# A larger memset behind each scattered DMA until the last rows are placed, and a waited small one per tile after that, in a mixture-of-experts kernel

## The chip, the cores and the metric

The kernel runs on one core of one Trainium2 chip. The metric is the device time of one execution in microseconds (us). Engines are named as the profile names them: PE is TensorE (PEld its weight loads), DVE VectorE, ACT ScalarE, POOL GpSimd, SP SyncE.

## What is computed

x is (16, 512, 512): 8192 tokens of 512 numbers. Cut to what matters, the reference is

```
z1 = einsum('bfi,bir->bfr', x, v) / 512          # low rank 16, per batch
z  = einsum('bfr,bor->bfo', z1, u) / 16
g  = gelu(einsum('bfi,oi->bfo', x, W) + fc_bias + z + b)
prob = softmax(g @ w_router + b_router)          # 16 experts
mask = the 4 largest of prob
h  = relu(einsum('nd,ebd->neb', g, w1b) + b1b)   # 16 blocks of 128
y  = einsum('neb,ebd,ne->nd', h, w2b, mask) + b2
return x + y
```

So each token goes through 4 of 16 experts, 32768 pairs of token and expert in all.

## The kernel before

**Stages.** The 8192 tokens are 16 batches (`b`) of 4 groups (`q`) of 128 tokens. Step `s = 4 * b + q` computes the first layer of one group on PE, GELU on ACT into a row buffer (`grow`, or a part of `ys`), and the router for it; DVE works out for every token its four places in per-expert lists (`ix`). POOL then sends the group's 128 rows to the lists in DRAM (`xg`) by four scattered (indirect) DMAs, one for each choice: `place_rows`, L476. A small table in DRAM, written by POOL's `place_tiles` (L488), says which expert and which rows make up the next full tiles of 512 rows.

**Tiles.** There are 72 tiles: 49 full ones and 23 made of two halves of 256 rows each, the last with one half. SP loads tile `j` (`load_tile`, L314) as `gr<-xg` together with its table entry `tabi<-table`, once the rows of all batches that the tile may need are in DRAM and the table is written. For tile 1 these are batches 0 to 4, for tiles 45 to 48 all 16 batches. The loops of all engines run over the same steps `s`; with `LAG = 28` tile `j` is computed in step `j + 28`: PE transposes it (L1171), multiplies it by the expert's w1 (L1186, L1191) and, one step later, by w2 (L1214). The results of chunks 0 and 2 of a tile are copied out by ACT (L650), those of 1 and 3 by DVE (L932), and POOL scatters each chunk of 128 rows to `yt` in DRAM: `send`, L504. Results rotate through 2 to 5 buffers (`ys`, `stx`, `grow`); a buffer is written again when the scatters of its last tile have landed (`s_y`). In the same way GELU waits with a row buffer until its last rows have landed (`s_sc`).

**What sets POOL's order.** POOL's loop (L516 to L532) is written out by hand. In step `s` it places the rows of group `s - 7` (four DMAs) and sends tile `s - 30` (four DMAs); up to step 30, and from step 67 on, the rows come first, otherwise the tile. The last rows (group 63) are placed in step 70, in which tile 40 is sent. Behind each of these DMAs stands `rest()` (L469): a memset of `pace`, 128 partitions by 16 floats. Its result is used by nobody. It waits on the semaphore `g_pace` until the memset before it is complete. The DMAs of `place_tiles` have no memset behind them.

**Expert weights late in the kernel.** From step 66 to step 73 ACT and DVE split the w2 of two experts a step into a high and a low part (`presplit_w2`, L902, L906). The low parts go to `w2l`, 16 x 512 floats on each partition, whose first eight and rows 12 to 14 serve other ends before. Row 15 is not used before its own split, the last.

**The end.** When all results are in DRAM, the four parts of each token are loaded (`xs<-yt`, `w2l<-yt`) and summed by DVE with the input and the bias, and the output is stored.

Of the kernel before, what the change touches and what calls it, by code (L numbers as in the profile page):

```python
# [9 lines left out]
NE = 16  # L10
KC = D // P
TOPK = 4
# [6 lines left out]
SLOTS = 4 * NB  # L19
LAG = 28  # L20
# [12 lines left out]
MORE = 39, 43, 55  # L33
EARLY = 12
AHEAD = EARLY + 8

ALU = mybir.AluOpType
ACT = mybir.ActivationFunctionType
AX = mybir.AxisListType
F32 = mybir.dt.float32  # L40
# [62 lines left out]
def result_buffer(j):  # L103
    return RESULT_BUFFER[j]
# [41 lines left out]
def adaln_ffn(nc, xT, xrow, fvT, fuT, cond, fc, wT, wrT, br, w1T, b1T, w2T, b2R, outT):  # L146
    with ExitStack() as ctx:
        def sb(name, shape, dt):
            return ctx.enter_context(nc.sbuf_tensor(name, shape, dt))

        def sem(name):
            return ctx.enter_context(nc.semaphore(name))
# [10 lines left out]
        w2l = sb("w2l", [P, NE, D], F32R)  # L163
# [97 lines left out]
        g_z, g_id, g_up, g_tok, g_k, g_s, g_pace = (  # L261
            sem(n) for n in ("g_z", "g_id", "g_up", "g_tok", "g_k", "g_s", "g_pace"))
# [166 lines left out]
        def _(pool):  # L429
# [37 lines left out]
            paced = [0]  # L467

            def rest():  # L469

                if paced[0] > 0:
                    pool.wait_ge(g_pace, paced[0])
                pool.memset(pace[:, :], 0.0).then_inc(g_pace, 1)  # L473
                paced[0] += 1

            def place_rows(b, q):  # L476
                pool.wait_ge(v_ix, b + 1)
                j = 4 * (b - RING + 3) - 1
                if j >= 0:
                    pool.wait_ge(s_gr[j % 2], 32 * (j // 2 + 1))  # L480
                    pool.wait_ge(s_gr[1 - j % 2], 32 * ((j - 1) // 2 + 1))
                for k in range(TOPK):
                    pool.indirect_dma_start(  # L483
                        out=xg, out_offset=bass.IndirectOffsetOnAxis(ap=ix[:, row_buffer(b), q, k:k + 1], axis=0),
                        in_=grows[row_buffer(b)][:, q, :], in_offset=None).then_inc(s_sc[row_buffer(b)][q], 16)
                    rest()
# [17 lines left out]
            def send(j, c):  # L504

                if c % 2 == 0:
                    pool.wait_ge(a_y, 2 * j + c // 2 + 1)
                else:
                    pool.wait_ge(v_y, 2 * j + c // 2 + 1)
                pool.indirect_dma_start(  # L510
                    out=yt, out_offset=bass.IndirectOffsetOnAxis(ap=ids[:, j % 8, c:c + 1], axis=0),
                    in_=yss[result_buffer(j)][:, c, :], in_offset=None, bounds_check=ROWS * TOPK - 1,
                    oob_is_err=False).then_inc(s_y[result_buffer(j)], 16)
                rest()

            for s in range(LAG + NTILE + 2):  # L516
                b, q = divmod(s, 4)
                j = s - LAG - 2
                first = s <= LAG + 2 or SLOTS + 3 <= s
                if 0 <= s - 7 < SLOTS and first:  # L520
                    place_rows((s - 7) // 4, (s - 7) % 4)
                if 0 <= j < NTILE:
                    for c in range(chunks(j)):
                        send(j, c)
                if 0 <= s - 7 < SLOTS and not first:
                    place_rows((s - 7) // 4, (s - 7) % 4)
                if q == 0 and 2 <= b <= NB:
                    place_tiles(b - 2)
                if s == 4 * (NB + 1) + 1:
                    place_tiles(NB - 1)  # L530
                if s == 4 * (NB + 1) + 4:
                    place_tiles(NB)  # L532
# [176 lines left out]
        def _(dve):  # L709
# [192 lines left out]
            def presplit_w2(e):  # L902

                dve.wait_ge(p_w, SLOTS)
                dve.wait_ge(a_p2, e + 1)
                dve.tensor_tensor(w2l[:, e, :], w2f[:, e, :], w2h[:, e, :].bitcast(F32), ALU.subtract).then_inc(v_p2, 1)  # L906

            def split_w2(j, e):
# [25 lines left out]
            def with_bias(i):  # L934
                dve.wait_ge(s_xr[i % len(xin)], 16 * (i // len(xin) + 1))
                x = xin[i % len(xin)]
                chain[0] += 1
                dve.tensor_tensor(x, x, b2f[:, :].unsqueeze(1).broadcast_to([P, 2, D]), ALU.add).then_inc(v_k, 1)

            def total(i):  # L940

                x, y = xin[i % len(xin)], yin[i % len(yin)]
                dve.wait_ge(s_yin[i % len(yin)], 16 * (i // len(yin) + 1))
                if i > 0:
                    dve.wait_ge(v_sum, 2 * i)
                for h in range(2):
                    chain[0] += 1
                    dve.tensor_tensor(two[:, 2 * h:2 * h + 2, :], y[:, 4 * h:4 * h + 2, :], y[:, 4 * h + 2:4 * h + 4, :],  # L948
                                      ALU.add).then_inc(v_k, 1)
                dve.wait_ge(v_k, chain[0])  # L950
                dve.tensor_tensor(x, x, two[:, 0:4:2, :], ALU.add).then_inc(v_sum, 1)
                dve.wait_ge(v_sum, 2 * i + 1)
                if i >= 4:
                    dve.wait_ge(s_out[i % 4], 16 * (i // 4))
                dve.tensor_tensor(ys[:, i // 2 % 2, i % 2 * 2:i % 2 * 2 + 2, :], x, two[:, 1:4:2, :],
                                  ALU.add).then_inc(v_sum, 1)
# [33 lines left out]
            for s in range(LAG + NTILE + 1):  # L990
                b, q = divmod(s, 4)
                j = s - LAG
# [43 lines left out]
                if SLOTS + 2 <= s < SLOTS + 2 + NE // 2:  # L1036
                    for e in range(2):
                        presplit_w2(2 * (s - SLOTS - 2) + e)
# [4 lines left out]
                if SLOTS + 19 <= s < SLOTS + 19 + EARLY:  # L1043
                    with_bias(s - SLOTS - 19)
            for i in range(EARLY, AHEAD):
                with_bias(i)
            for i in range(NSUM - 1):
                total(i)
                if i + AHEAD < NSUM:
                    with_bias(i + AHEAD)  # L1050
            for h in range(2):
# [238 lines left out]
```

## Time and profile before

| what | us |
|---|---|
| median of 3 runs | 1123.3 |
| lowest, highest | 1121.24, 1125.75 |
| the profiled execution | 1120.76 |
| its span, first to last instruction | 1118.8 |

Of the span PE is busy 77%, DVE 74%, POOL 58% and ACT 52%. The busy share of an engine is an average over stages that have different limits, so it must be read by stage. Five stages can be told apart in the trace: up to 42 us nothing is scattered yet; from 42 to about 165 us rows are placed and no tile is computed; to about 600 us rows are placed and tiles computed together; to about 676 us the last rows go out; to about 903 us there are only tiles; and the rest is the final sum. Times of the trace count from the start of the span. The granted clock of TensorE is given as a share of its full speed.

### The profile page before, as it was taken

How to read it: one execution, taken by the hardware profiler on the slowest of the kernel's cores; microseconds unless marked ns; L12 is line 12 of the kernel's file. 1: busy time of each engine (PE TensorE's matmuls, PEld its weight loads, DVE VectorE, ACT ScalarE, POOL GpSimd, SP SyncE). 2: the span in 40 equal slices, each digit the busy share in tenths (PEclk: the TensorE clock that was granted, in tenths of full speed). 3: DMA queues.
4: the chain of work that ended last, by engine and by line, in shares of the span. 5: the costliest groups of instructions: out<-in, count | busy, mean ns of one | idle time of the engine just before them, and what ended most of it. 6: DMA issues, size and time to landing. Idle time of an engine off the chain costs nothing.

```text
span 1118.8 us, 18458 instructions
## 1 busy us (share of the span) xinstructions
PE 863.2 (77%) x4924; PEld 675.3 (60%) x4924; DVE 826.5 (74%) x1964; ACT 580.9 (52%) x1061; POOL 652.8 (58%) x1131
## 2 busy tenths in 40 slices
PE   8999969999999999999999889999999910000000
PEld 7777747777787777778777667777777710000000
DVE  4565647777767767777768888768888769877787
ACT  6555637566676667667567677666666600000000
POOL 1488875777777777877778888556666530000000
PEclk9999979999999999999999999999999965555555
DMA  6798788898888989899879889889887599999999
GB/s 192 246 361 328 267 300 280 295 317 308 304 305 302 331 297 311 312 310 312 300 273 322 318 308 354 255 291 323 273 282 234 169 357 417 431 424 431 427 432 387
DMA packets 103238, 354.85 MB, mean 317 GB/s; under 512 B 29961, under 2 KB 29961, under 8 KB 92384
## 3 DMA queue, kind: packets, MB, share of 16 engines
q1 hardware_dynamic: 59104, 217.21, 56.3%
q0 software_dynamic: 43936, 136.37, 31.1%
q8 instruction: 41, 0.67, 0.3%
q14 instruction: 61, 0.50, 0.2%
q10 hardware_dynamic: 96, 0.10, 0.0%
HBM read 200.47 MB, written 169.65 MB: 331 GB/s over the span
## 4 chain that ended last, share of the span: by engine, by line
PE 55%; DMA 16%; POOL 10%; DVE 8%; issue 4%; ACT 4%; ACTq 1%; DVEq 1%; SPq 0%; POOLq 0%
PE yps L1214 12%; PE lay L1081 12%; DMA w2l<-yt 11%; PE hid L1186 11%; PE trn L1171 8%; POOL xg L483 7%; PE hid L1191 5%; PE trn L1101 2%; DVE stx L948 2%; PE hid L1067 2%; DMA outT<-ys 2%; POOL yt L510 2%; DMA tabi<-table 2%; ACT w1c L604 1%; PE rps L1116 1%
## 5 line engine op out<-in xcount | busy, mean ns | idle before, releaser
L510 POOL DMA_INDIRECT yt<-ys,ids x218 | 233.4, 1071 | 120.7 <-ACT ys L650 74.4
L757 DVE TENSOR_TENSOR gsb<-trn,gsb 128x512 fp32r<-128x512 f32 x286 | 191.1, 686 | 130.4 <-ACT gsb L591 129.5
L483 POOL DMA_INDIRECT xg<-grow,ix x224 | 224.0, 1000 | 80.4 <-DVE ix L831 42.0
L1171 PE MATMUL trn<-idf,gr 128*128 128x128 f32 x1144 | 178.5, 280 | 24.9 <-DVE gsb L757 13.8
L1081 PE MATMUL lay<-w2l,xs 128*128 128x512 f32 x768 | 191.3, 398 | 0.0
L1171 PEld LDWEIGHTS trn<-idf,gr 128*128 128x128 f32 x1144 | 136.4, 142 | 80.0 <-DVE gsb L757 44.6
L591 ACT ACTIVATE gsb<-trn 128x512 fp32r<-128x512 f32 x286 | 170.9, 598 | 21.9 <-PE trn L1171 21.7
L1081 PEld LDWEIGHTS lay<-w2l,xs 128*128 128x128 f32 x768 | 142.7, 190 | 29.7
L1214 PE MATMUL yps<-w2c,hh 128*128 128x512 f32 x368 | 132.1, 440 | 4.1 <-issue 4.1
L1186 PE MATMUL hid<-gsb,w1c 128*128 128x512 f32 (+1 forms) x576 | 129.9, 368 | 0.3
L619 ACT ACTIVATE hv<-hid,b1c 128x512 f32<-128x512 f32 (+1 forms) x94 | 52.6, 584 | 138.5 <-PE hid L1191 137.6
L1186 PEld LDWEIGHTS hid<-gsb,w1c 128*128 128x128 f32 x576 | 93.3, 189 | 21.4 <-DVE w2c L898 5.2
L932 DVE COPY ys<-yps 128x512 f32<-128x512 f32 x109 | 74.1, 680 | 3.8 <-PE yps L1214 2.3
L473 POOL MEMSET pace<- 128x16 f32 x542 | 75.6, 140 | 0.1
L1214 PE MATMUL yps<-w2c,hl 128*128 128x512 f32 x184 | 73.1, 397 | 0.0
L574 ACT ACTIVATE grow<-lay 128x512 f32<-128x512 f32 x56 | 33.5, 597 | 72.2 <-PE lay L1086 50.4
L650 ACT ACTIVATE ys<-yps 128x512 f32<-128x512 f32 x109 | 65.6, 602 | 7.4 <-PE yps L1214 4.9
L1191 PE MATMUL hid<-gsb,w1c 128*128 128x512 f32 (+1 forms) x288 | 67.6, 357 | 0.0
L898 DVE TENSOR_TENSOR w1c<-w1f,w1c 128x512 fp32r<-128x512 f32 x72 | 49.5, 687 | 13.9 <-ACT w1c L604 11.9
L1214 PEld LDWEIGHTS yps<-w2c,hh 128*128 128x128 f32 x368 | 55.9, 192 | 5.9 <-issue 5.3
L510 POOL DMA_INDIRECT yt<-stx,ids x40 | 44.3, 1108 | 22.8 <-ACT stx L650 10.7
L1191 PEld LDWEIGHTS hid<-gsb,w1c 128*128 128x128 f32 x288 | 49.5, 189 | 8.1
(185 smaller groups left out, 1535.2 us busy)
## 6 DMA issues: line engine op xcount, KB each, us to landing
gr<-xg SPq DMA_DIRECT2D x49, 1056.0 KB
xs<-yt SPq DMA_DIRECT2D x16, 2048.0 KB, 19.5
w2l<-yt SPq DMA_DIRECT2D x15, 2048.0 KB, 19.5
gr<-xg SPq DMA_DIRECT2D x45, 528.0 KB
stx<-xT SPq DMA_DIRECT2D x64, 256.0 KB, 3.6
outT<-ys SPq DMA_DIRECT2D x31, 512.0 KB, 20.4
xg<-xrow SPq DMA_DIRECT2D x16, 528.0 KB, 6.8
w2f<-xrow SPq DMA_DIRECT2D x16, 512.0 KB, 13.0
```

The lines of the kernel that those rows point to most:

```text
L473: pool.memset(pace[:, :], 0.0).then_inc(g_pace, 1)
L483: pool.indirect_dma_start(out=xg, out_offset=bass.IndirectOffsetOnAxis(ap=ix[:, row_buffer(b), q, k:k + 1], axis=0), in_=grows[row_buffer( ...
L510: pool.indirect_dma_start(out=yt, out_offset=bass.IndirectOffsetOnAxis(ap=ids[:, j % 8, c:c + 1], axis=0), in_=yss[result_buffer(j)][:, c, ...
L591: act.activation(gsb[:, :, HI, c * P:(c + 1) * P], trn[n % 2][:, :].rearrange("p (k t) -> p k t", k=KC), ACT.Copy).then_inc(a_tn, 1)
L650: act.activation(yss[result_buffer(j)][:, c, :], yps[c % 2][:, :], ACT.Copy).then_inc(a_y, 1)
L757: dve.tensor_tensor(gsb[:, :, LO, c * P:(c + 1) * P], trn[n % 2][:, :].rearrange("p (k t) -> p k t", k=KC), gsb[:, :, HI, c * P:(c + 1) * ...
L932: dve.tensor_copy(yss[result_buffer(j)][:, c, :], yps[c % 2][:, :]).then_inc(v_y, 1)
L1081: pe.matmul(lay[s % 2][:, :], xs[:, b % 2, k, h, cols], wls[:, k, a, :], start=(k == 0 and a == HI and h == HI), stop=False)
L1171: last = pe.transpose(trn[n % 2][:, k * P:(k + 1) * P], gr[:, j % 2, c, k * P:(k + 1) * P], idf[:, :])
L1186: pe.matmul(hid[:, cols], w1x[h][:, a, k * P:(k + 1) * P], gsb[:, k, HI, cols], start=(h == 0 and k == 0 and a == HI), stop=False)
L1191: last = pe.matmul(hid[:, cols], w1x[h][:, HI, k * P:(k + 1) * P], gsb[:, k, LO, cols], start=False, stop=(h == len(parts) - 1 and k == KC ...
L1214: last = pe.matmul(yps[c % 2][:, :], hx[:, c * P:(c + 1) * P], w[a], start=(i == 0), stop=(i == 2))
```

## The change

`rest()` now clears another piece of memory: columns 0 to 255 of row 15 of `w2l`, that is 256 floats on each of 128 partitions in place of 16. It stands behind each scatter of `place_rows` and behind those of tiles 0 to 40. For tiles 41 to 71 there is no `rest()`. In its place a new function `stop()` stands behind chunk 1 of each tile: the old memset of 16 floats, and then a wait of POOL itself for its completion. Since `w2l` row 15 is written by `presplit_w2` for expert 15, DVE waits there for all 420 memsets of `rest()` (4 x 64 of rows, 4 x 41 of tiles).

```
+PACED = SLOTS + 7 - LAG - 2
+REST = 256
@@ rest()
                 if paced[0] > 0:
                     pool.wait_ge(g_pace, paced[0])
+                pool.memset(w2l[:, NE - 1, 0:REST].bitcast(F32), 0.0).then_inc(g_pace, 1)
+                paced[0] += 1
+
+            def stop():
+
                 pool.memset(pace[:, :], 0.0).then_inc(g_pace, 1)
                 paced[0] += 1
+                pool.wait_ge(g_pace, paced[0])
@@ send(j, c)
-                rest()
+                if j < PACED:
+                    rest()
+                elif c == 1:
+                    stop()
@@ presplit_w2(e)
                 dve.wait_ge(a_p2, e + 1)
+                if e == NE - 1:
+                    dve.wait_ge(g_pace, TOPK * SLOTS + 4 * PACED)
```

POOL's order changes only from tile 41 on. This is POOL at the end of tile 40 and in tile 41, before. A row is one instruction with what it writes and reads; in brackets are the semaphores it waits for, `a_y` from ACT's copy, `v_y` from DVE's.

```order
L510 DMA yt<-stx,ids 32768x512 [waits v_y]
L473 MEMSET pace 128x16 [waits g_pace]
L510 DMA yt<-ys,ids 32768x512 [waits a_y]
L473 MEMSET pace 128x16 [waits g_pace]
L510 DMA yt<-ys,ids 32768x512 [waits v_y]
L473 MEMSET pace 128x16 [waits g_pace]
L510 DMA yt<-ys,ids 32768x512 [waits a_y]
L473 MEMSET pace 128x16 [waits g_pace]
L510 DMA yt<-ys,ids 32768x512 [waits v_y]
L473 MEMSET pace 128x16 [waits g_pace]
```

The same place after; L475 is the memset of `rest()`, L480 that of `stop()`, L518 the scatter of `send`.

```order
L518 DMA yt<-stx,ids 32768x512 [waits v_y]
L475 MEMSET w2l 128x256 [waits g_pace]
L518 DMA yt<-ys,ids 32768x512 [waits a_y]
L518 DMA yt<-ys,ids 32768x512 [waits v_y]
L480 MEMSET pace 128x16
L518 DMA yt<-ys,ids 32768x512 [waits a_y,g_pace]
L518 DMA yt<-ys,ids 32768x512 [waits v_y]
L518 DMA yt<-ys,ids 32768x512 [waits a_y]
```

No DMA has moved; the large memset still stands behind tile 40, and of tile 41's four memsets one is left, for which the next DMA now waits.

On DVE the last two splits of w2 stand one behind the other at the end of step 73, before:

```order
L916 TENSOR_TENSOR hl<-hv,hh 128x512 [waits a_hh]
L906 TENSOR_TENSOR w2l<-w2f,xs 128x512 [waits a_p2,p_w] x2
L910 REGISTER_ALU [waits a_w2]
L910 TENSOR_TENSOR w2c<-w2f,w2c 128x512
L766 TENSOR_TENSOR above<-gr,tabi 128x12 [waits s_y_1,s_gr_0]
```

And after:

```order
L929 TENSOR_TENSOR hl<-hv,hh 128x512 [waits a_hh]
L919 TENSOR_TENSOR w2l<-w2f,xs 128x512 [waits a_p2,p_w]
L919 TENSOR_TENSOR w2l<-w2f,xs 128x512 [waits g_pace,a_p2,p_w]
L923 REGISTER_ALU [waits a_w2]
```

Nothing moved on DVE; the second split of this pair waits for `g_pace` too.

## Rows read from the trace of the kernel before

**Rows 1.** Busy time by stage: us, then each engine's busy time (instructions).

```profile
core 0: us, PE busy (x) PEld busy (x) DVE busy (x) ACT busy (x) POOL busy (x), PEclk, DMA share, GB/s
42.00:165.00 123.00, 111.62 (x624) 81.86 (x623) 68.05 (x293) 63.92 (x110) 104.37 (x181) 0.96 0.87 311
165.00:600.00 435.00, 433.79 (x2417) 341.24 (x2418) 317.11 (x906) 291.32 (x528) 329.86 (x577) 0.99 0.89 305
600.00:676.00 76.00, 65.91 (x343) 51.01 (x344) 65.49 (x177) 53.27 (x97) 65.51 (x113) 0.98 0.87 321
676.00:903.00 227.00, 213.82 (x1324) 170.70 (x1322) 179.26 (x377) 147.10 (x287) 145.41 (x228) 1.00 0.82 273
```

**Rows 2.** Chain of work that ended last, 120 to 182 us: start, us, what.

```profile
140.20 1.13 POOL xg L483
...
150.44 0.97 POOL xg L483
151.71 3.21 DMA xg<-grow,ix
155.20 0.34 SPq L339
155.60 7.58 DMA tabi<-table
...
165.95 1.97 PE trn L1171 x8
```

**Rows 3.** The same chain, 595 to 680 us.

```profile
599.54 5.48 DMA tabi<-table
605.11 0.98 POOL yt L510
...
659.79 3.12 DMA xg<-grow,ix
663.71 6.54 DMA tabi<-table
670.29 0.66 PE trn L1171 x4
```

**Rows 4.** POOL alone, scatters of rows (L483): us, busy (instructions).

```profile
42.00:151.80 109.80, 79.90 (x80) 0.96 0.88 316
165.00:600.00 435.00, 143.13 (x144) 0.99 0.89 305
605.10:659.90 54.80, 23.45 (x24) 0.97 0.87 328
```

**Rows 5.** POOL alone, scatters of results (L510), same columns.

```profile
165.00:600.00 435.00, 143.27 (x140) 0.99 0.89 305
605.10:659.90 54.80, 17.90 (x17) 0.97 0.87 328
```

**Rows 6.** POOL's timeline: start us, us, what [idle before <-releaser].

```profile
63.05 0.97 POOL L483 DMA_INDIRECT xg<-grow,ix  x1 [0.18 <-issue]
64.01 0.17 POOL L473 MEMSET pace<- 128x16 f32 x1
64.32 0.97 POOL L483 DMA_INDIRECT xg<-grow,ix  x1
65.28 0.13 POOL L473 MEMSET pace<- 128x16 f32 x1
65.59 0.97 POOL L483 DMA_INDIRECT xg<-grow,ix  x1 [0.18 <-issue]
...
677.13 1.28 POOL L500 DMA_INDIRECT table<-tval,thalf  x1 [0.18 <-issue]
678.72 0.89 POOL L500 DMA_INDIRECT table<-tval,thalf  x1 [0.30 <-issue]
679.92 1.01 POOL L510 DMA_INDIRECT yt<-grow,ids  x1 [0.30 <-issue]
```

**Rows 7.** POOL's timeline at the start of the kernel, the same columns.

```profile
0.74 0.20 POOL L430 MEMSET idf<- 128x128 f32 x1 [0.29 <-POOLq L1283]
0.88 0.20 POOL L431 MEMSET upper<- 128x128 bf16 x1
1.02 0.11 POOL L432 MEMSET base<- 128x16 bf16 x1
1.07 0.10 POOL L433 MEMSET tzero<- 128x4 int32 x1
```

**Rows 8.** POOL's waits, 180 to 600 us: waited for, us in total, times, longest.

```profile
POOL yt L510 <- ACT ys L650: 47.0, 52, 4.8
POOL xg L483 <- DVE ix L831: 5.2, 9, 0.6
POOL yt L510 <- DVE ys L932: 2.2, 2, 1.3
```

**Rows 9.** POOL's timeline: the last memset that the change enlarges.

```profile
665.92 0.14 POOL L473 MEMSET pace<- 128x16 f32 x1
```

**Rows 10.** DVE's splits of w2 and copies of results: ns min/median/max, first to last start.

```profile
L906 DVE TENSOR_TENSOR w2l<-w2f,xs x16: 678/684/742, 618.4 to 685.9; 128x512 fp32r<-128x512 f32 x16
...
L932 DVE COPY ys<-yps x109: 669/680/691, 179.4 to 901.8; 128x512 f32<-128x512 f32 x109
```

**Rows 11.** A long scatter on POOL beside DVE's work.

```profile
70.61 0.69 DVE L735 TENSOR_TENSOR xs<-stx,xs 128x512 fp32r<-128x512 f32 x1
...
70.68 1.46 POOL L483 DMA_INDIRECT xg<-grow,ix  x1 [0.18 <-issue]
```

**Rows 12.** POOL's last scatters.

```profile
897.84 0.99 POOL L510 DMA_INDIRECT yt<-stx,ids  x1 [0.23 <-issue]
...
904.74 1.97 POOL L510 DMA_INDIRECT yt<-ys,ids  x1 [0.18 <-issue]
```

## The prediction

> **What bounds the kernel now.** I read the busy time by stage first [rows 1], then the chain of work that ended last, in order of time [rows 2, 3], then POOL's own timeline [rows 6]. From 165 to 600 us PE is busy 433.8 of 435 us: PE is the bound, and POOL, with 330 us busy and 54 us of waits for ACT and DVE (47.0 + 5.2 + 2.2) [rows 8], follows it. The same holds from 676 to 903 us: PE 214 of 227 us, POOL 145. In two stretches POOL sets the pace. In the first, 42 to 151.7 us, it issues 80 scatters of rows with hardly a gap [rows 4]; the 80th, at 151.71, is the last of batch 4, and the chain goes from it through its landing to the load of a tile and to PE at 165.95 [rows 2]. In the second, 605.1 to 659.8 us, it issues 24 + 17 scatters [rows 4, 5], and the chain goes from the last rows at 659.79 to the tile load and PE at 670.3 [rows 3]. After 903 us there is only the final sum. So what one scatter costs more on POOL is paid about 80 + 41 = 121 times, and elsewhere only beyond POOL's waits.
>
> **The larger memset.** The question is what stands between two scatters. With a memset between them, the second starts 0.30 us after the first has ended: 64.32 + 0.97 = 65.29, next start 65.59 [rows 6]. Without a memset, between the two table writes at 677.13 and 678.72, it is 0.31, and 0.30 from the second to the scatter behind it [rows 6]. So a memset of 16 floats costs nothing now: the gap is 0.30 us with it or without it, and the memset lies inside. It ends 0.13 us after the scatter (64.32 + 0.97 = 65.29 to 65.28 + 0.13 = 65.41), and the 0.18 us that follow are called "issue". One row says whether the next scatter is held by the end of the memset. At 64.01 a memset took 0.17 us, and ended 0.16 us after its scatter, 0.03 late; the next scatter still started at 64.32, 0.30 after the scatter, with 0.14 us behind the memset and not 0.18 [rows 6]. The start follows the scatter, not the memset, at least that far.
>
> How long is the new one? The memset of 128 floats at 0.74 lets the next start 0.14 us later, that of 16 floats at 1.02 lets the next start 0.05 later [rows 7]. That is 0.09 us for 112 floats, or 0.8 ns for each. From 16 to 256 floats it is 240 x 0.83 = 0.20 us more: the engine is held about 0.25 us and the memset ends about 0.13 + 0.20 = 0.33 us after the scatter. The gap is 0.30 us.
>
> The bounds of its cost, for each scatter:
> - Lowest, 0: the next scatter needs the engine only at the end of the gap, 0.30 us, and the memset holds it for 0.25. Memsets already start before the one ahead has ended (0.88 against 0.74 + 0.20) [rows 7], so an end at 0.33 need not hold back a start at 0.30. Below nothing is excluded: the gap without any memset is the same, so no memset can shorten it.
> - If the scatter waits for the memset's end and starts at once: 0.33 - 0.30 = 0.03, times 121 = 3.6 us.
> - Highest: the scatter needs the 0.14 us behind the memset's end which the row at 64.32 still shows. 0.33 + 0.14 - 0.30 = 0.17 us, times 121 = 20.6 us.
>
> I take 0 to 0.03, and of it the lower end, since two rows (the equal gaps, the late memset) speak against a scatter that waits for the memset, and none for it: **0 to 3.6 us, taken as 0.5**. Between the stretches the 284 scatters (144 + 140) [rows 4, 5] would need more than 54 / 284 = 0.19 us each before POOL became the bound there; even the highest bound is just under that. What covers the memset is the 0.30 us gap; were it gone, the price would be the highest bound.
>
> Beside this, the Trainium skill (GPSIMD Engine Reference, section 2.1, Instruction dispatch) says that completion of a POOL instruction gates what waits on its semaphore and does not hold back the next POOL instruction, but that each of the engine's cores starts an instruction when it has finished its share of the one before. By its first half the late memset of the trace is as it should be. By its second half the extra 0.20 us would stand in line on the cores that write the descriptors, as the serial rival below has it, and then the 0.05 us that 16 floats hold the engine should show between the gaps with and without a memset, which they don't.
>
> **Who else sees the memset.** DVE's copies of results take 669 to 691 ns, a spread of 0.02 us, over 109 of them [rows 10], so nothing of POOL's holds them. A scatter is long (1.46 in place of 0.97) where it starts inside a DVE operation with both inputs in SBUF [rows 11]; the memset reads nothing and doesn't move the starts, so these collisions stay. DVE's new wait: memset number 420 is the one behind the last chunk of tile 40, at 665.92 [rows 9], and the split that waits for it is the last, at 685.9 [rows 10]. It has 20 us in hand; cost 0. What would queue behind it if it weren't met is the split of tile weights and all of tile 46 on DVE.
>
> **From tile 41 on.** 122 memsets go (30 tiles of four chunks and one of two) and 31 come. Taking one away gains nothing, by the equal gap. The new wait holds POOL until the small memset is complete (0.13 us after the scatter), and only then is the next scatter let go. Nothing in this trace shows a scatter behind such a wait. Its lowest price is 0, if the memset's end still falls inside the 0.30 us; its highest 0.13, if the gap of 0.30 begins anew at the memset's end. I take the highest, for 31 tiles. What queues behind it are chunks 2 and 3 of the tile and the next tile; who waits for these are ACT and DVE for a result buffer. POOL has 227 - 145 = 82 us idle or in gaps there [rows 1] and each tile takes some 8.5 us of PE, so 0.13 us a tile is hidden but at the very end. There the last six scatters run nearly back to back from 897.84 to 904.74 [rows 12]; in them stands one stop that delays the last scatter (that of tile 70; the one behind tile 71's chunk 1 comes after it) and one just ahead. That is 0.1 to 0.3 us on the end; I take **0.2**.
>
> **Sum.** 0.5 + 0.2 = 0.7 us on the profiled execution: 1120.8 + 0.7 = 1121.5. The profiled execution lies 2.5 us under the median of the runs, so for a median: 1123.3 + 0.7 = **1124.0 us**.
>
> **Rivals.**
> 1. *The memset is served in line* (slower). The scatter starts a fixed time behind the memset's end, 0.14 to 0.18 us [rows 6], wherever that falls. For it: this is how the timeline reads in nearly every row ("0.18 issue"). Against it: the gap without a memset, and the row at 64.32. It costs 0.17 to 0.20 us a scatter: 121 x 0.17 = 20.6 to 121 x 0.20 = 24 us, and from 0.19 on also the middle stage, where 284 x 0.20 = 57 us meet 54 us of waits that can't all be absorbed, some 3 to 10 us. Time: **1144 to 1157 us**. It makes the kernel measurably slower from 0.047 us a scatter (5.6 / 121); partial cover, say 0.05 to 0.15, gives 1129 to 1142.
> 2. *Fewer collisions* (faster). If the starts shift after all, the long scatters may fall elsewhere. In the stretch from 605 to 660 us they add about 2 us, in the first some 3 (POOL was busy 79.9 us for 80 scatters where 80 x 0.97 = 77.6 would do [rows 4]). All gone: 1119. More than 0.5% can't be had from this, so a time under 1117.7 would need something that no row shows, say transfers that suffer less when their scatters stand apart. The DMA engines are 87 to 89% busy in these stages [rows 1], which leaves it room.
> 3. *The stop matters*: POOL restarts slowly after each wait, with more than 2 us a tile. Then the stage to 903 us would grow by the excess. POOL's slack of 82 us for 27 tiles makes this improbable; 31 x 0.13 = 4 us are far from it. Time if it did with 0.5 us a tile: still 1124.
> 4. *The change doesn't do what it says*: the wait of DVE for 420 memsets binds. It would need POOL 20 us later than DVE against now; in rival 1 POOL's delay shifts DVE too. No time of its own.
>
> **How the numbers follow.** No cost worth measuring (1117.7 to 1129, this forecast): 0.60. Rival 1 whole: 0.18. Rival 1 in part: 0.12. Faster by something unseen: 0.10. A measurement of this kernel can tell about 0.5%, 5.6 us, from no change. Hence faster 0.10, same 0.60, slower 0.30. The range goes from 1117, which leaves out most of the faster cases (0.08), to 1150, which takes in the partial cases and the lower half of rival 1 and leaves out 0.10. The forecast's own range is 1120 to 1128.
>
> **What would show it.** Right: in the timeline of the changed kernel the large memset ends some 0.33 us behind its scatter and the next scatter starts at 0.30 to 0.33; the 80th scatter of rows starts within 3 us of 151.7, the last within 4 us of 659.8. Rival 1: scatters 0.47 to 0.50 apart, the 80th near 165 to 168. The stops: 0.30 to 0.45 us between chunk 1 and chunk 2 from tile 41 on, and no wait of DVE for POOL before the last split of w2. What would make it wrong: a next scatter that needs the memset's end plus a fixed time, or a memset slower than 0.8 ns a float when it stands behind a scatter.

## The result and the profile after

| | before | after |
|---|---|---|
| median of 4 runs each, us | 1124.52 | 1160.7 |
| the profiled execution, us | 1120.76 | 1161.33 |
| its span, us | 1118.8 | 1159.5 |

The changed kernel takes 1.032 times as long (95% interval 1.030 to 1.035), 36 us more; its runs lie between 1158.9 and 1163.84. The forecast was 1124, with a range of 1117 to 1150: wrong, and outside the range. The two profiled executions differ by 40.6 us, since that of before lies 3.8 us under the median of this comparison.

The stages, cut in both traces at the same scatters: the first of rows, the 80th of rows (the last of batch 4), the 144th of results (that at 605.11 in [rows 3]), the last of rows and the last of results. Columns as in [rows 1], whose cuts lie elsewhere. First before, then after.

```profile
42.02:151.71 109.69, 100.61 (x575) 73.72 (x574) 62.56 (x278) 58.30 (x101) 94.06 (x163) 0.97 0.89 317
151.71:605.11 453.40, 449.89 (x2493) 353.44 (x2493) 326.29 (x930) 299.62 (x541) 344.38 (x603) 0.99 0.88 304
605.11:659.79 54.68, 48.01 (x252) 37.36 (x252) 48.47 (x133) 39.72 (x72) 47.23 (x81) 0.97 0.88 329
659.79:904.74 244.95, 226.61 (x1390) 180.26 (x1388) 194.31 (x413) 157.95 (x307) 161.04 (x255) 1.00 0.82 276
```

```profile
43.28:166.42 123.14, 110.55 (x616) 81.05 (x614) 67.38 (x283) 62.81 (x108) 108.55 (x164) 0.96 0.80 282
166.42:633.73 467.31, 447.80 (x2475) 350.88 (x2476) 327.48 (x931) 297.43 (x541) 409.15 (x602) 0.98 0.86 297
633.73:696.02 62.29, 46.16 (x236) 35.30 (x236) 47.92 (x144) 37.79 (x68) 55.38 (x82) 0.92 0.75 275
696.02:945.51 249.49, 226.60 (x1380) 180.59 (x1380) 193.71 (x400) 156.54 (x303) 148.20 (x163) 0.98 0.80 273
```

In the second stage PE was idle for 3.5 us before and is now idle for 19.5 us, and POOL is busy 409 of 467 us. What happened to POOL stands in its timeline (start us, us, what, idle before and its releaser), against [rows 6]:

```profile
59.71 0.97 POOL L491 DMA_INDIRECT xg<-grow,ix  x1 [0.16 <-issue]
60.67 0.33 POOL L475 MEMSET w2l<- 128x256 f32 x1
61.16 0.97 POOL L491 DMA_INDIRECT xg<-grow,ix  x1 [0.16 <-issue]
62.13 0.33 POOL L475 MEMSET w2l<- 128x256 f32 x1
```

A scatter ends (59.71 + 0.97), the memset runs for 0.33 us, and the next scatter starts 0.16 us behind it: 0.49 us from end to start, where it was 0.30. The chain of waits in the first stretch, which was scatters and their gaps in [rows 2], now contains the memsets as well (start, us, what):

```profile
164.96 0.97 POOL xg L491
165.93 0.33 POOL w2l L475
166.25 0.17 issue
166.42 2.74 DMA xg<-grow,ix
...
179.97 1.97 PE trn L1184 x8
```

Its later part, against [rows 3]:

```profile
616.10 4.59 DMA tabi<-table
620.69 0.97 POOL yt L518
...
633.73 1.46 POOL yt L518
...
696.02 3.24 DMA xg<-grow,ix
700.05 7.26 DMA tabi<-table
```

The tile load at 616.10 is not the one at 599.54 before: POOL issues 48 scatters from it to the last rows, where it issued 41. So the start times of the same scatters locate the loss:

| scatter | before | after | later by |
|---|---|---|---|
| first of rows | 42.02 | 43.28 | 1.3 |
| 80th of rows | 151.71 | 166.42 | 14.7 |
| 144th of results | 605.11 | 633.73 | 28.6 |
| last of rows | 659.79 | 696.02 | 36.2 |
| last of results | 904.74 | 945.51 | 40.8 |

Each line holds what the lines above it have lost: 13.5 us go in the first stretch, 13.9 in the middle stage, 7.6 with the last 41 scatters, 4.5 among the tiles. The 1.3 us mean nothing: in the ten traces of kernels that ran at this speed the first scatter starts at 41.9 to 44.8 us. The last 4.5 mean little: that stretch takes 244.8 to 248.8 us in `f7`, `f8` and `f9` below, which have the same small memsets there. The stops are in it too; they are priced alone below.

### The profile page after: what moved, and what is told of

Its sections match the earlier page's. It is cut to its first block, busy times and chain, and to the rows that moved or that the text cites. A ratio compares the mean times of both kernels' runs of the same rounds, so it can differ in the third digit from the quotient of the medians.

```text
span 1159.5 us, 18398 instructions
## 1 busy us (share of the span) xinstructions
PE 869.5 (75%) x4924; PEld 678.2 (58%) x4924; DVE 829.3 (72%) x1964; ACT 580.0 (50%) x1061; POOL 727.3 (63%) x1040
## 4 chain that ended last, share of the span: by engine, by line
POOL 39%; PE 24%; DMA 16%; issue 8%; DVE 7%; ACT 4%; ACTq 1%; DVEq 1%; POOLq 0%; SPq 0%
POOL xg L491 17%; POOL yt L518 11%; DMA w2l<-yt 11%; POOL w2l L475 9%; PE hid L1199 6%; PE yps L1227 5%; PE lay L1094 4%; PE trn L1184 3%; PE hid L1204 3%; DVE stx L961 2%; DMA outT<-ys 2%; DMA tabi<-table 2%; ACT w1c L615 1%; DMA xg<-grow,ix 1%; DVE ys L968 1%
## 5 line engine op out<-in xcount | busy, mean ns | idle before, releaser
L518 POOL DMA_INDIRECT yt<-ys,ids x218 | 233.1, 1069 | 86.5 <-issue 32.4
L1184 PE MATMUL trn<-idf,gr 128*128 128x128 f32 x1144 | 181.4, 283 | 54.0 <-DMA tabi<-table 31.8
L475 POOL MEMSET w2l<- 128x256 f32 x420 | 142.3, 339 | 0.1
L518 POOL DMA_INDIRECT yt<-stx,ids x40 | 45.0, 1125 | 28.4 <-DVE stx L945 13.8
## 6 DMA issues: line engine op xcount, KB each, us to landing
xs<-yt SPq DMA_DIRECT2D x16, 2048.0 KB, 19.5
w2l<-yt SPq DMA_DIRECT2D x15, 2048.0 KB, 19.5
```

Source lines behind the costliest of these rows:

```text
L475: pool.memset(w2l[:, NE - 1, 0:REST].bitcast(F32), 0.0).then_inc(g_pace, 1)
L518: pool.indirect_dma_start(out=yt, out_offset=bass.IndirectOffsetOnAxis(ap=ids[:, j % 8, c:c + 1], axis=0), in_=yss[result_buffer(j)][:, c, ...
L1184: last = pe.transpose(trn[n % 2][:, k * P:(k + 1) * P], gr[:, j % 2, c, k * P:(k + 1) * P], idf[:, :])
```

## The experiments

**Which half of the change.** `e1_large_only` has the large memset and not the stops: from tile 41 on the old small memset stands behind each scatter.

```diff
+            def small_rest():
+
+                pool.wait_ge(g_pace, paced[0])
                 pool.memset(pace[:, :], 0.0).then_inc(g_pace, 1)
                 paced[0] += 1
-                pool.wait_ge(g_pace, paced[0])
...
                 if j < PACED:
                     rest()
-                elif c == 1:
-                    stop()
+                else:
+                    small_rest()
```

> The large memset (256 floats) stands behind the rows and tiles 0 to 40 as in the changed kernel; from tile 41 on the small memset of the kernel before stands behind every scatter, and nothing waits for it on POOL. Theory A, the next scatter starts 0.17 us behind the end of the memset whatever its length: the scatter pitch up to tile 40 is 1.46 us in place of 1.27 and nearly all of the 36 us stay, 1156 to 1160 us. Theory B, the waited stop behind chunk 1 of each tile is what costs (the changed trace has gaps of 0.8 to 0.9 us behind it): then this kernel falls back to 1124 to 1135 us. A splits the total: what is missing to 1160.7 is the price of the stop, by the last scatters of the trace 1.5 to 4 us.

1160.79 us against 1124.57, ratio 1.032 (1.030 to 1.035): the whole loss.

`e2_stop_only` has the stops and leaves `rest()` as it was.

> The other part alone: the small memset of the kernel before up to tile 40, then the waited small memset behind chunk 1 of each tile and none behind the others. Theory A (the large memset is the cause): 1124 to 1128 us, the stops costing only on the last tiles. Theory B (the stop is the cause): 1150 to 1160 us. Both expect a gap of 0.9 us behind each stop in place of 0.30.

1126.14 us, ratio 1.0013 (1.0001 to 1.0026): 1.6 us. (With no large memset, DVE's wait before the last split is left out as well.) The stop itself is longer than the forecast's 0.30 to 0.45 us. POOL's timeline of the changed kernel at tile 41:

```profile
705.00 0.98 POOL L518 DMA_INDIRECT yt<-ys,ids  x1 [0.30 <-issue]
705.96 0.15 POOL L480 MEMSET pace<- 128x16 f32 x1
706.90 0.98 POOL L518 DMA_INDIRECT yt<-ys,ids  x1 [0.79 <-POOL pace L480]
```

From the end of the scatter at 705.98 to the next start at 706.90 are 0.92 us. Over the 30 stops of this trace that a scatter follows the gap is 0.90 to 1.20 us, with a median of 1.10, so 0.6 to 0.9 more than a plain one. POOL has the time for it, as forecast.

`e3_no_memset` has no memset and no stop behind any scatter (`rest()` returns at once).

> No memset behind any scatter. If a memset of 16 floats is hidden in the 0.30 us between scatters, as the rows with and without one say, the scatters keep a pitch of 1.27 us and the time stays within 0.3% of 1124.5 us. If it costs its own 0.13 us (theory A taken to its end: what the next scatter waits for is the end of whatever stands before it), the pitch falls to about 1.14 us and the time to 1105 to 1112 us. If the memset was of use for something that no row shows (spacing the transfers), the time goes up.

1124.03 us, ratio 0.9989 (0.9973 to 1.0005): the same. Its scatters start 1.26 us apart, with a gap of 0.30:

```profile
60.03 0.96 POOL L480 DMA_INDIRECT xg<-grow,ix  x1 [0.30 <-issue]
61.29 0.96 POOL L480 DMA_INDIRECT xg<-grow,ix  x1 [0.30 <-issue]
```

**How the gap depends on the memset.** `e4_ladder` puts eleven sizes behind the scatters of rows and of tiles 0 to 40 in turn, so that each size stands in every stage up to there.

```diff
+LADDER = 0, 4, 16, 32, 64, 96, 128, 192, 256, 384, 512
...
+                size = LADDER[turn[0] % len(LADDER)]
+                turn[0] += 1
+                if size == 0:
+                    return
                 if paced[0] > 0:
                     pool.wait_ge(g_pace, paced[0])
-                pool.memset(w2l[:, NE - 1, 0:REST].bitcast(F32), 0.0).then_inc(g_pace, 1)
+                pool.memset(w2l[:, NE - 1, 0:size].bitcast(F32), 0.0).then_inc(g_pace, 1)
```

> Behind the scatters up to tile 40 the size of the memset goes in turn through none, 4, 16, 32, 64, 96, 128, 192, 256, 384 and 512 floats; later as in the changed kernel. It gives the gap between two scatters against the size. Theory A: gap = end of the memset + 0.17 us, and from 16 floats on 0.83 ns a float: 0.32 at 32, 0.34 at 64, 0.37 at 96, 0.40 at 128, 0.45 at 192, 0.50 at 256, 0.61 at 384, 0.72 at 512. Theory C, a fixed window with the memset inside and the engine held only by what goes over it: 0.30 up to some size, then a slope of 0.83 ns a float, so that at 256 floats 0.19 us are over the window and the bend lies near 30 floats. A gap in steps, or one that doesn't grow evenly, would speak for a third: something polled at intervals.

1140.46 us, one run. What it was made for is POOL's timeline:

```profile
94.27 0.97 POOL L497 DMA_INDIRECT xg<-ys,ix  x1 [0.17 <-issue]
95.54 0.96 POOL L497 DMA_INDIRECT xg<-ys,ix  x1 [0.30 <-issue]
...
99.51 0.14 POOL L481 MEMSET w2l<- 128x32 f32 x1
99.82 0.97 POOL L497 DMA_INDIRECT xg<-ys,ix  x1 [0.16 <-issue]
100.79 0.17 POOL L481 MEMSET w2l<- 128x64 f32 x1
101.11 0.97 POOL L497 DMA_INDIRECT xg<-ys,ix  x1 [0.16 <-issue]
...
109.54 0.97 POOL L497 DMA_INDIRECT xg<-ys,ix  x1 [0.16 <-issue]
110.51 0.54 POOL L481 MEMSET w2l<- 128x512 f32 x1
111.22 0.97 POOL L497 DMA_INDIRECT xg<-ys,ix  x1 [0.17 <-issue]
```

The medians over all scatters behind each size, from the end of one scatter to the start of the next, in ns:

| floats | none, 4, 16, 32 | 64 | 96 | 128 | 192 | 256 | 384 | 512 |
|---|---|---|---|---|---|---|---|---|
| memset ends behind the scatter | 117 (4), 128 (16), 140 (32) | 167 | 194 | 221 | 274 | 328 | 435 | 542 |
| gap | 305 | 325 | 358 | 385 | 439 | 492 | 599 | 706 |

Two straight pieces: the gap is 0.305 us, or the memset's end plus some 0.164 us (0.158 at 64 floats, 0.164 to 0.165 from 96 on), whichever is later. The memset costs 0.83 ns a float. The two meet near 32 to 40 floats. With 16 floats the memset's side is 0.128 + 0.164 = 0.292 us, an estimate: it was hidden, but with little more than 0.013 us to spare. The gap with and without the memset was equal because the two sides are nearly equal, and not because a scatter has nothing to do with the memset.

**What the scatter waits for.** `e5_upper_half` and `e6_lower_quarter` are `e1_large_only` with the memset on partitions 64 to 127 and 0 to 31 only (`w2l[64:P, ...]`, `w2l[0:32, ...]`).

> As the kernel with the large memset alone, but its 256 floats are cleared on partitions 64 to 127 only. The time of the memset per partition is the same, and so is the moment of its completion. Theory D, the next scatter waits for the completion of the memset as a whole: gap 0.49 us as before, time 1155 to 1160 us. Theory E, only the part of the engine that serves the low partitions is needed by a scatter and the memset stands in line just there: gap 0.30 us and about 1124 us.

> The 256 floats are cleared on partitions 0 to 31 only. Theory D (completion) and theory E (in line in the part of the engine for low partitions) both expect a gap of 0.49 us and 1155 to 1160 us; if the cost comes from the total written (256 x 128 floats against 256 x 32), the gap falls to about 0.35 us and the time to 1130 us.

```profile
61.05 0.33 POOL L475 MEMSET w2l<- 64x256 f32 x1
61.55 0.97 POOL L491 DMA_INDIRECT xg<-grow,ix  x1 [0.16 <-issue]
```

The row is of the first: 0.33 us and a gap of 0.49, as with 128 partitions; so too with 32. In these three cases neither the number of partitions nor their place matters, only the floats of a partition. Here the scatter has no wait on `g_pace`, and yet starts 0.16 us behind the end of the memset. The Trainium skill (GPSIMD Engine Reference, section 2.1, Instruction dispatch) says that completion gates what waits on the instruction's semaphore and does not hold back the next POOL instruction, but that each core starts an instruction when it has finished its share of the one before. By the first half alone the scatter would not follow the memset, and it does. By the second half it would, in both runs, if it needs cores from both ranges of partitions; whether it does, or whether the engine waits for the memset as a whole, no run here shows. The times of these two belong to the section on the second kind of chip, below: they ran, with the next two, on a chip on which the kernel before takes 1329.8 us.

**Where it is paid.** The large memset in one part of the kernel alone, the small one everywhere else, no stops. Steps 0 to 30 (100 scatters, with the 80 of the first stretch) and steps 31 to 64 (the middle stage, for which the forecast found enough waits to cover up to 0.19 us a scatter):

```diff
-                pool.memset(w2l[:, NE - 1, 0:REST].bitcast(F32), 0.0).then_inc(g_pace, 1)
+                (pool.memset(w2l[:, NE - 1, 0:REST].bitcast(F32), 0.0) if LAG + 2 < step[0] <= 64
+                 else pool.memset(pace[:, :], 0.0)).then_inc(g_pace, 1)
```

For the first stretch the condition is `step[0] <= LAG + 2`. Beside them ran a copy of the changed kernel, and `e1_large_only` with 56 floats in place of 256.

> The changed kernel itself once more, since the kernel before took 1330 us in one job, on another chip, in place of 1124 us, and kernels with the large memset 1249 to 1308 us there. If the chip is like the first ones: 1161 us against 1124. If it is like the slow one: 1245 to 1260 against 1330, and the sign of the change depends on the chip.

> The large memset up to step 30 only, repeated because the other job was on a chip where the kernel before took 1330 us. On a chip with 1124 us for the kernel before: the 80 scatters cost 80 x 0.187 = 15 us, 1138 to 1141 us, or less if the middle stage catches up.

> The large memset in steps 31 to 64 only, repeated for the same reason. By the prediction's working 1124 to 1130 us (waits of POOL cover 54 us); by the debt that comes due where the last rows are placed 1134 to 1140 us. With f7 and the last stretch (41 x 0.187 = 8 us) the sum should come to 36 us.

> The memset that stands behind rows and tiles 0 to 40 has 56 floats in place of 256. By the ladder the next scatter starts at 0.305 us or 0.164 us behind the memset's end, whichever is later; at 56 floats the two meet (0.305 to 0.325 us). So a memset 3.5 times the old one costs nothing to 0.015 us a scatter: within 0.2% of the kernel before (1123 to 1127 us), where a cost in proportion to size (36 us x 40 / 240) would give 1130.

| | us (before: 1125.25) | ratio, interval |
|---|---|---|
| f1_after | 1160.0 | 1.032 (1.028 to 1.035) |
| f7_large_to_30 | 1138.19 | 1.011 (1.009 to 1.014) |
| f8_large_31_to_64 | 1137.05 | 1.011 (1.008 to 1.014) |
| f9_size_56 | 1124.92 | 1.0005 (0.998 to 1.003) |

The first stretch costs 12.9 us and the middle stage 11.8 us; of the 34.8 us of `f1_after` some 10 are left for the steps from 65 on, the stops with them, by subtraction only (their 48 scatters times 0.187 would be 9). 56 floats cost nothing that can be measured. The median of their gap is 0.318, 0.013 us more than before, and 121 of them would be 1.6 us; a price in proportion to the floats added would have been near 6.

How the middle stage pays stands in the waits. The first large memset of f8_large_31_to_64 starts at 193.36 us. POOL's waits for ACT and DVE from 193.4 to 600 us (waited for, us in total, times, longest), in the kernel before and then in f8_large_31_to_64:

```profile
POOL yt L510 <- ACT ys L650: 39.7, 49, 1.1
POOL xg L483 <- DVE ix L831: 5.2, 9, 0.6
POOL yt L510 <- DVE ys L932: 0.9, 1, 0.9
```

```profile
POOL yt L520 <- ACT ys L664: 0.6, 1, 0.6
POOL yt L520 <- DVE ys L948: 0.5, 2, 0.3
```

ACT's for rows to land, 180 to 600 us, in the same order:

```profile
ACT grow L574 <- DMA xg<-grow,ix: 21.6, 11, 2.9
```

```profile
ACT grow L588 <- DMA xg<-grow,ix: 79.4, 27, 6.7
```

The stage has 272 scatters with a large memset (34 steps of eight), 272 x 0.187 = 51 us. The waits that could cover it were 45.8 us; the other 8.6 of the 54.4 in [rows 8] lie before the first large memset. They are gone but for 1.1 us: POOL has become the bound of the middle stage. Counted over the same scatters, from the 80th of rows to the 144th of results, the trace has 51 us more of gaps, 6.7 us more in the scatters themselves, table writes included (313.8 against 307.1) and 42.4 us less of waits, and the stage is 15.0 us longer (468.4 against 453.4). GELU's row buffers come free later, so that ACT waits 58 us more for them, and from 180 to 600 us PE is busy 412.3 us with 2289 matmuls where it was 419.7 us with 2351.

The loss is paid scatter by scatter within the stage. In f8_large_31_to_64 the 80th scatter of rows starts at 153.21 us, as in `e2_stop_only` at 153.25; the 101st is 1.2 us later than there, the 141st 6.7, the 181st 9.4 and the 233rd 15.4. Behind the stage, with small memsets again, nothing is added: the last rows start at 676.75 against 661.86.

**Another kind of chip.** On three chips, those of the e5 to e8, g and h runs, the unchanged kernel takes 1330 us, 18% more, and there the changed kernel is faster. No chip is on record at both speeds, so a kind of chip can't be told from a condition that a chip was in; "kind" stands for either.

The expectations of the e runs were written in view of a kernel before of 1124 us.

> The large memset only up to step 30, that is behind the rows that are placed before and with tile 0 and behind tile 0; small ones after that. If each stretch pays by itself: the 80 scatters before the first tile loads cost 80 x 0.19 = 15 us: 1138 to 1141 us. If a late start is caught up by the slack of the middle stage: under 1130 us.

> The large memset only in steps 31 to 64, where PE was the bound in the kernel before. By the working of the prediction (284 scatters x 0.19 = 54 us against 54 us of waits) it costs next to nothing, 1124 to 1130 us. By the changed trace, in which the last rows go out 36 us later though the first stretch gave 15 and the last 41 scatters 8, POOL falls behind in the middle and the debt comes due where the last rows are placed: 1134 to 1140 us.

> The changed kernel, now on whichever chip this is. Where the kernel before takes 1124 us: 1160 us. Where it takes 1330 us: theory F, there a dense row of scatters on POOL holds up the other engines (in that job's traces DVE and ACT stood idle for 9 to 13 us and went on within 0.5 us of the end of POOL's row), and the longer memset lets them in: 1245 to 1260 us. If it isn't the spacing that helped there: near 1330.

> No memset at all. Where the kernel before takes 1124 us: 1124 again. Where it takes 1330 us: by theory F the gap between scatters is what matters, and it is 0.305 us with the small memset and without, so again 1320 to 1340 us; if the memset itself is what lets the others in, slower than with the small one, over 1345.

> The large memset from step 65 to tile 40 only. The stretch up to the last rows holds some 46 scatters of which 41 were on the chain: 41 x 0.187 = 7.7 us, 1132 to 1134 us where the kernel before takes 1124. With 12.9 us (up to step 30) and 11.8 us (31 to 64) from the other two parts the sum would be 32 to 33 of 36 us; more than 10 us here would close it.

> The kernel before, for its trace on this chip. On a chip like the slow ones (1330 us): the first stretch near 142 us (first to 80th scatter of rows), the tiles at 9.2 to 9.6 us each. On a chip like the others: 110 us and 8.5 us, 1124 us.

> The stops alone. Where the kernel before takes 1124 us: 1126 again. Where it takes 1330 us: by theory F a stop opens a gap of 0.9 us in each tile's row of four scatters, the other engines keep up, and the tile stage falls from 275 to 252 us as in the changed kernel there: 1300 to 1310 us, the stretches before it unchanged.

> The changed kernel with 512 floats in place of 256: by the ladder a gap of 0.706 us, 0.40 more than with 16 floats. Where the kernel before takes 1124 us: POOL is the bound up to the last rows, 0.215 us more for each of some 400 scatters that can't be absorbed any more, 1235 to 1250 us. Where it takes 1330 us: by theory F POOL's rows no longer hold the others up at all and POOL's own pitch is what is left: also 1235 to 1260 us, so that 256 is about the best size there.

`g3_large_from_65` has the large memset for steps from 65 on (`64 < step[0]`), `h3_size_512` is the changed kernel with `REST = 512`; the other edits are those of the same names above, and `h1_before` is a copy of before.

| | us | before | ratio, interval |
|---|---|---|---|
| g1_after | 1224.07 | 1331.04 | 0.920 (0.914 to 0.926) |
| h3_size_512 | 1249.04 | 1330.66 | 0.938 (0.933 to 0.944) |
| e5_upper_half | 1248.88 | 1329.8 | one run |
| e6_lower_quarter | 1254.29 | 1329.8 | one run |
| e8_large_31_to_64 | 1284.83 | 1329.8 | 0.965 (0.958 to 0.972) |
| h2_stop_only | 1308.14 | 1330.66 | 0.985 (0.977 to 0.993) |
| e7_large_to_30 | 1308.52 | 1329.8 | 0.983 (0.976 to 0.990) |
| g3_large_from_65 | 1317.12 | 1331.04 | 0.991 (0.987 to 0.995) |
| g2_no_memset | 1317.96 | 1331.04 | 0.990 (0.986 to 0.994) |
| h1_before | 1330.28 | 1330.66 | 0.999 (0.996 to 1.003) |

Each part gains: 21, 45, 14 us for the large memset by stages, 23 for the stops, together 103 of the 107 us of `g1_after`. That the sum comes so near is partly luck: each part is uncertain by 6 to 11 us, and they are from three chips. The expectations missed `g1_after` (1245 to 1260) and, by 2 us, `g2_no_memset` (1320 to 1340), and that of `h2_stop_only` has the right time for a reason that holds in part only: from the last rows to the last results 263 us against 284, not 252. The memset as such doesn't help (without any it is 13 us better than with the small one, at the same gap of 0.305 us); the gap does, also where a stop and not a long memset makes it, and up to some size, since 512 floats are worse than 256. POOL's scatters and gaps are equal to 0.01 us on both kinds of chip. What differs is seen in the timeline of `h1_before`, in a dense row of scatters:

```profile
53.98 0.64 PE L1116 MATMUL rps<-stx,wrz 128*32 128x256 f32 x8
...
60.70 0.97 POOL L483 DMA_INDIRECT xg<-grow,ix  x1 [0.18 <-issue]
61.67 0.13 POOL L473 MEMSET pace<- 128x16 f32 x1
61.98 0.97 POOL L483 DMA_INDIRECT xg<-grow,ix  x1 [0.18 <-issue]
62.47 0.75 DVE L785 TENSOR_SCALAR fu<-rps,brc 128x512 f32<-128x512 f32 x1 [9.19 <-remote]
...
63.27 1.89 PE L1125 MATMUL rps<-sumk,fu 128*128 128x16 f32 x8 [8.07 <-DVE fu L785]
```

DVE's input was there at 54.62 (53.98 + 0.64); DVE starts 7.9 us later, and PE waits for DVE. "remote" is what the profile says where no instruction of the core is seen to release it. In `g1_after`, on the same kind of chip, the same instruction follows its input at once:

```profile
53.68 0.64 PE L1129 MATMUL rps<-stx,wrz 128*32 128x256 f32 x8
...
54.38 0.75 DVE L796 TENSOR_SCALAR fu<-rps,brc 128x512 f32<-128x512 f32 x1 [1.41 <-issue]
```

ACT's largest group of waits of this kind over the span (us in total, times, longest), in `h1_before` and then in `g1_after`:

```profile
ACT hv L619 <- remote: 108.2, 28, 5.9
```

```profile
ACT hv L630 <- remote: 21.1, 9, 3.4
```

All such waits of ACT and DVE together are 265 us in `h1_before`, 143 in `g1_after` and 0.2 in `h3_size_512`, and none in any of the ten traces from the first kind of chip. In `h1_before` 55 of them are longer than 2 us, 245 us together. 185 us of that lie inside rows of three or more scatters with plain gaps, which fill some 55% of the time, and 36 of the 55 end 1 to 2 us behind the end of such a row. This speaks for something that the other engines need and that is held up on the second kind while POOL issues scatters densely, and that wider gaps let through. With 512 floats it is gone, and what is left is POOL's own pitch: POOL makes up 41% of the chain that ended last there, and 0% in `g1_after`. This explains why 512 floats are worse than 256.

What it is that is held up, the traces don't say. The DMA engines had room (0.79 busy in the middle stage of `g1_after`, 0.71 in that of `h1_before`; columns as in [rows 1]):

```profile
180.00:760.00 580.00, 493.65 (x2539) 379.44 (x2538) 335.45 (x957) 312.22 (x554) 352.26 (x616) 0.93 0.71 245
```

TensorE's clock accounts for a part at most: PE is busy 917 us in `h1_before` and 863 before, for as many matmuls at a mean granted clock of 0.865 against 0.895, where the times differ by some 200 us. Whether it is the fetch of instructions, the delivery of semaphores or something else stays open.

## Why the prediction was wrong

**The price of the large memset, the term that failed.** Taken 0.5 us, measured 36. Three things went into it.

The *length* was right: "the memset ends about 0.13 + 0.20 = 0.33 us after the scatter", measured 0.328. (The row of [rows 7] at 1.02 is of 16 bf16 numbers and not of floats, and 0.09 us for 112 of them are 0.80 ns and not the 0.83 of the sum; neither changes the result, and the row at 0.88 shows that the type made no difference.)

The *choice between the bounds* was wrong. Highest bound 0.17 us a scatter, measured 0.187, just above it. The two witnesses for the lower end were weak. The equal gap with and without a memset can't tell a scatter that ignores the memset from one that waits for it and finds it done in time; at 0.292 against 0.305 us it was the latter. To tell them apart takes a memset whose end plus the usual distance lies clearly outside 0.305, and the trace had one such row only, that at 64.01 in [rows 6], with a distance of 0.14 in place of 0.18 us. That row was read as a rule. It is the only one of the kernel's 541 gaps with less than 0.17 us behind the memset, and the ladder's medians are 0.158 at 64 floats and 0.164 to 0.165 from 96 on, so the row was a stray one. Nearly every row said "0.18 issue" behind a memset; the prediction wrote that down under its first rival, and gave it 0.18.

The *number of scatters that pay* was wrong too: "elsewhere only beyond POOL's waits", with 54 / 284 = 0.19 us each as the cover of the middle stage. Of the 54.4 us only 45.8 lie where the large memsets of that stage are, 0.16 us a scatter, which is under the 0.187 that each costs; and the scatters themselves took longer. So POOL became the bound there, and the stage that was put at nothing paid 11.8 us alone and 13.9 in the trace of the changed kernel. The other two terms came out as counted: 80 scatters times 0.187 = 15 us, against 12.9 measured alone and 13.5 in the trace, and the last 41 scatters 7.7 us, against 7.6 in the trace.

**The first rival** was the mechanism. It asked for 1144 to 1157 us and for the 80th scatter "near 165 to 168"; measured 1160.7 and 166.42. Its upper end missed by 4 us, of which 2 to 4 are the middle stage, to which it gave only 3 to 10 us. The range was cut at 1150 in the middle of it.

**What was right.** The stop is hidden but at the end: 1.6 us alone, against 0.2 taken, though its size was missed: 0.6 to 0.9 us and not 0.13 (the bound "0.13 if the gap begins anew" was no bound, since no row showed POOL behind a wait for its own memset). With 31 of them and 82 us of idle time in that stage a size some five to seven times larger changed next to nothing. DVE's wait costs nothing: memset 420 came at 703.20 and the last split at 724.7, so there were still 21 us.

```profile
703.20 0.34 POOL L475 MEMSET w2l<- 128x256 f32 x1
```

```profile
L919 DVE TENSOR_TENSOR w2l<-w2f,xs x16: 677/686/748, 643.4 to 724.7; 128x512 fp32r<-128x512 f32 x16
```

The fourth rival's guess that DVE shifts with POOL holds. The small memset's cost of zero is confirmed by `e3_no_memset`, the absence of contention by DVE's splits (686 ns after, 684 before, [rows 10]). Long scatters, the second rival, are about as many as before: 88 of 542 take more than 1.1 us, against 89.

**What the prediction could not know** is the second kind of chip. The forecast gave 0.10 to a gain from something unseen, transfers or engines that suffer less when the scatters stand apart. It exists, with 8%, on chips that the time before of 1123.3 us excluded.

## What to carry to other kernels

Equal times with and without a small piece of work show that it fits under something, not how much room is left: before enlarging it, work out both sides of the "later of the two" from single rows, and take the side that nearly every row shows against the one that a single row shows. The waits of an engine cover a cost only where the cost falls: count them from the first place at which it is paid, and set them against the upper bound of the price. Once they are used up that engine is the bound of a stage that was another's. And where a change moves how densely one engine issues its transfers, run it on more than one chip before calling it a loss or a gain.

## What the runs showed of the hardware that was not expected

- Behind a scatter, a memset of n floats on each partition ends 0.117 (4) to 0.542 us (512) later, 0.83 ns a float, for 32, 64 or 128 partitions alike; the next scatter starts at the later of 0.305 us and that end plus 0.158 to 0.165 us.
- A wait of POOL for its own memset gives a gap of 0.90 to 1.20 us between scatters, where the memset without the wait gives 0.305.
- Two kinds of chip (or conditions of one): the same kernel takes 1124 to 1125 us or 1330 us. On the second, DVE and ACT stand idle for up to 9 and 11 us at a time, mostly during dense scatters (`h1_before`), and wider gaps on POOL (0.49 us) make the kernel 8% faster; on the first they make it 3% slower.
- No one version is best on both. On the first kind nothing that ran beats the kernel before (`e3_no_memset` and `f9_size_56` are the same), on the second the changed kernel is the fastest.
